# A two-layer kernel on one core: the opening's queues in another order

## The chip, the cores and the metric

The kernel runs on one core of a Trainium2 chip. The core's engines are TensorE (PE), VectorE (DVE), ScalarE (ACT), GpSimd (POOL) and SyncE (SP); each works through a queue of its own in order, and they meet at semaphores. The metric is the device time of one execution in microseconds; lower is better.

## The reference

Sixteen batches of x, each 512 rows of 512 columns, go through two layers with a residual each. Here is what is computed, cut to what matters:

```python
# layer 1, on h = layernorm(x); ctx is 16 x 512 x 1024
h = rmsnorm(h, g_res); h = einsum('bld,ed->ble', h, W_in) + b_in
h_patch = rmsnorm(ctx, g_init)[..., :512]
s = associative_scan(decay, h_patch)                    # a short-lived decay: a**k, a about 0.001
plug = clip(cumsum(boundary_mask(patch_lens)) - 1, 0, plen - 1)
x = x + s[plug] + h
# layer 2, on y = layernorm(x)
y_prev = y shifted by one row
xr = mu_r * y + (1 - mu_r) * y_prev;  xk = mu_k * y + (1 - mu_k) * y_prev
out = x + sigmoid(xr @ W_r.T) * (square(relu(xk @ W_k.T)) @ W_v.T)
```

## The kernel before

Every matrix is kept as a high part and a low part (`_hi`, `_lo`), and each product is three TensorE matmuls (lines 484 to 486): high by high and the two mixed ones. ScalarE makes the high part by a copy (`copy`, L704), VectorE the low part by a subtraction (`low`, L894). The host hands over x twice, in rows and turned (`in_x_turned`), so that the first projection needs no transposes.

A batch has four row tiles `t` and four column chunks `c` of 128. For a batch b the stages are: load of turned x (`xt`) and of x (`ring[b.slot]`, three buffers), their high and low parts (`x_hi`, `x_lo`), the projection with W_in (`project_tile`), the scan of the context rows (`stats_c`, `scan_input`, `u_high`, `u_low`, `scan`, `scan_out`), the store of the scan to the DRAM tensor `s_rows` (`store_scan`, from ScalarE's queue), then four indirect DMAs from POOL that add rows of `s_rows` to x (`add_rows`, L426, semaphores `dep_added`), then `add_x` (L1019), the statistics and the norm (`stats_b`, `norm_b`), the turn by transposes (`turn`, L588), the mixing with the previous row, and the gate, key and value products with W_r, W_k and W_v.

The loop is software-pipelined: `iteration(b)` of each engine works on b, b+1 and b+2. Before it stands an opening, written out by hand at the end of each engine's function, with batch 0's first layer and the preparation of the weights. The orders in it are what the change touches. In the opening, POOL makes a table of powers of the decay with 13 selects for each of its two halves (`make_decay`, L363), TensorE sums the weights' columns (L681), counts boundary marks with 64 small matmuls (`count_marks`, L660) and sums them (`sum_marks`, L672), and VectorE centres W_in (`centre`, L1144), takes running sums of the marks (`running_marks`) and makes the row numbers for the indirect DMAs (`patches`).

W_in is staged in `gate`, W_r in `turned`, W_k in `ring[2]`, W_v in `gate` again. Turned x of batch 0 and of batch 1 both go to `xt`, so batch 1's load waits on SP until batch 0's low parts are made (`xt_lo_ready`), and W_r's load stands behind it. The iteration for b = -1 (`is_first(nxt)` on VectorE, `first_steps` on TensorE) adds up batch 0, projects batch 1 and turns batch 0. `far` is a branch that this data does not take: every engine in it loads a flag from `far_table` and jumps over.

## Time and profile before

| | us |
|---|---|
| median of 3 runs | 786.25 (785.98 to 786.61) |
| the profiled execution | 788.05 |
| its span, first to last instruction | 786.5 |
| PE busy | 756.9 (96%) |
| DVE busy | 553.8 (70%) |
| ACT busy | 413.3 (53%) |
| POOL busy | 173.4 (22%) |
| mean granted TensorE clock | 0.986 of 2.4 GHz |

The chain of the whole profiled execution puts 85% of the span on PE, 4% on DVE, 4% on POOL and 1% on DMA. A start time is counted from the first instruction. A reader looks for the stretches in which PE is not busy, for the engine that it waits for there, and follows that engine's queue back.

### The profile page before, as it was taken

The numbers are of one execution on the slowest core, as the hardware profiler recorded it, in microseconds if no ns is written. First come the engines' busy times: TensorE is split into PE (matmuls) and PEld (weight loads), VectorE is DVE, ScalarE is ACT, GpSimd is POOL, SyncE is SP. The second block draws the span as 40 slices with busy tenths as digits, with TensorE's granted clock in tenths as the row PEclk, the third lists the DMA queues.
The fourth block names the chain that finished last, engine by engine and source line by source line (L and its number), as shares of the span: only waits on it lengthen the run. The fifth ranks groups of instructions, "written<-read, shape, count | busy, mean of one in ns | idle before, by whom it ended". The sixth has DMA issues, their size and how long they took to land.

```text
span 786.5 us, 11081 instructions
## 1 busy us (share of the span) xinstructions
PE 756.9 (96%) x3462; PEld 624.1 (79%) x3463; DVE 553.8 (70%) x1005; ACT 413.3 (53%) x681; POOL 173.4 (22%) x175
## 2 busy tenths in 40 slices
PE   7669899999999999999999999999999999999997
PEld 4457688888888888888888888888888888888876
DVE  4678797685866868586686858667685867667452
ACT  3317755454654645466464546656454665544760
POOL 7244131311213131121313112131311213130000
PEclk9879999999999999999999999999999999999999
DMA  7476153441706244170624417062441706231011
GB/s 256 150 188 166 60 124 132 112 143 47 209 2 167 88 110 144 46 208 0 156 98 109 144 43 211 0 166 88 108 146 41 212 0 160 94 102 20 1 54 54
DMA packets 42765, 85.73 MB, mean 109 GB/s; under 512 B 3536, under 2 KB 3536, under 8 KB 42704
## 3 DMA queue, kind: packets, MB, share of 16 engines
q1 hardware_dynamic: 30624, 63.71, 21.7%
q0 software_dynamic: 9216, 16.78, 13.5%
q10 hardware_dynamic: 2880, 4.76, 1.7%
q14 instruction: 31, 0.25, 0.1%
q8 instruction: 14, 0.23, 0.1%
HBM read 64.26 MB, written 21.76 MB: 109 GB/s over the span
## 4 chain that ended last, share of the span: by engine, by line
PE 85%; DVE 4%; POOL 4%; issue 2%; ACT 2%; DMA 1%; DVEq 0%; POOLq 0%; ACTq 0%
PE bank L484 27%; PE bank L486 27%; PE bank L485 27%; PE bank L588 3%; POOL ring L426 2%; DMA s_rows<-scanned 1%; POOL decay L363 1%; DVE xk_lo L894 1%; DVE scratch L989 0%; DVE ring L1019 0%; DVE gate L1044 0%; ACT scratch L794 0%; POOL rs_a L389 0%; DVE bn_a L923 0%; DVE bn_b L1025 0%
## 5 line engine op out<-in xcount | busy, mean ns | idle before, releaser
L426 POOL DMA_INDIRECT ring<-s_rows,patch_now x60 | 99.4, 1656 | 245.8 <-DMA s_rows<-scanned 214.6
L894 DVE TENSOR_TENSOR xr_lo<-scratch,xr_hi 128x512 fp32r<-128x512 f32 x124 | 85.6, 690 | 68.9 <-ACT xr_hi L704 68.4
L989 DVE SCALAR_TENSOR_TENSOR scratch<-turned,cols,scratch 128x512 f32<-128x512 f32 x128 | 94.6, 749 | 34.4 <-ACT scratch L749 15.0
L484 PE MATMUL bank<-wi_hi,xt_hi 128*128 128x512 f32 x256 | 104.0, 406 | 5.1 <-DVE xt_lo L894 5.1
L704 ACT ACTIVATE turned<-bank 128x512 f32<-128x512 f32 x64 | 33.4, 604 | 143.3 <-PE bank L588 114.7
L484 PE MATMUL bank<-xk_hi,wk_hi 128*128 128x512 f32 x256 | 99.9, 390 | 2.2 <-DVE xk_lo L894 2.2
L485 PE MATMUL bank<-wi_lo,xt_hi 128*128 128x512 f32 x256 | 101.8, 398 | 0.0
L486 PE MATMUL bank<-wi_hi,xt_lo 128*128 128x512 f32 x256 | 101.5, 396 | 0.0
L484 PE MATMUL bank<-wr_hi,xr_hi 128*128 128x512 f32 x256 | 99.7, 389 | 0.8 <-DVE xr_lo L894 0.8
L486 PE MATMUL bank<-xk_hi,wk_lo 128*128 128x512 f32 x256 | 99.6, 389 | 0.0
L485 PE MATMUL bank<-xk_lo,wk_hi 128*128 128x512 f32 x256 | 99.6, 389 | 0.0
L486 PE MATMUL bank<-wr_hi,xr_lo 128*128 128x512 f32 x256 | 99.6, 389 | 0.0
L485 PE MATMUL bank<-wr_lo,xr_hi 128*128 128x512 f32 x256 | 99.6, 389 | 0.0
L484 PE MATMUL bank<-wv_hi,xr_hi 128*128 128x512 f32 x240 | 94.0, 392 | 2.7 <-DVE xr_lo L894 2.7
L486 PE MATMUL bank<-wv_hi,xr_lo 128*128 128x512 f32 x240 | 93.4, 389 | 0.0
L485 PE MATMUL bank<-wv_lo,xr_hi 128*128 128x512 f32 x240 | 93.4, 389 | 0.0
L749 ACT ACTIVATE scratch<-turned,cols 128x512 f32<-128x512 f32 x128 | 89.5, 711 | 0.5
L704 ACT ACTIVATE xr_hi<-scratch 128x512 fp32r<-128x512 f32 x124 | 77.9, 628 | 20.4 <-DVE scratch L989 17.7
L781 ACT ACTIVATE gate<-bank 128x512 f32<-128x512 f32 x64 | 37.5, 595 | 83.3 <-PE bank L486 83.3
L1044 DVE TENSOR_TENSOR gate<-bank,gate 128x512 f32<-128x512 f32 x64 | 43.6, 688 | 53.2 <-PE bank L486 51.2
L395 POOL TENSOR_TENSOR rs_b<-v_b,half 128x4 f32<-128x4 f32 x16 | 16.5, 1034 | 230.5 <-DVE v_b L1031 230.5
L704 ACT ACTIVATE xk_hi<-scratch 128x512 fp32r<-128x512 f32 x64 | 40.4, 632 | 47.6 <-DVE scratch L989 46.8
(131 smaller groups left out, 1283.5 us busy)
## 6 DMA issues: line engine op xcount, KB each, us to landing
ring<-in_x SPq DMA_DIRECT2D x16, 1024.0 KB, 7.4
out<-gate SPq DMA_DIRECT2D x64, 256.0 KB
xt<-in_x_turned SPq DMA_DIRECT2D x15, 1024.0 KB, 5.2
ctx_rows<-in_ctx SPq DMA_DIRECT2D x16, 512.0 KB, 8.0
s_rows<-scanned ACTq DMA_DIRECT2D x16, 256.0 KB, 2.0
gate<-in_L_xattn_W_in SPq DMA_DIRECT2D x4, 256.0 KB, 3.4
xt<-in_x_turned SPq DMA_DIRECT2D x2, 512.0 KB, 6.3
turned<-in_L_ffn_W_r SPq DMA_DIRECT2D x1, 1024.0 KB, 7.8
```

The source lines that it names most:

```text
L395: nc.gpsimd.tensor_tensor(rs_b[:, :, 0], v_b[:, :, 0], half[:, :], ALU.pow).then_inc(rs_b_done, 1)
L426: pool.indirect_dma_start(ring[b.slot][:, t, :], None, s_rows[:, :], bass.IndirectOffsetOnAxis(ap=rows, axis=0), compute_op=ALU.add).then_ ...
L484: nc.tensor.matmul(where, lhs_hi, rhs_hi, start=start, stop=False)
L485: nc.tensor.matmul(where, lhs_hi, rhs_lo, start=False, stop=False)
L486: return nc.tensor.matmul(where, lhs_lo, rhs_hi, start=False, stop=stop)
L588: last = nc.tensor.transpose(first_bank(b, t)[:, tile(c)], normed[:, t, c * P:(c + 1) * P], ident[:, :])
L704: return nc.scalar.activation(to, of, ACT.Copy)
L749: nc.scalar.activation(scratch[:, i % 2, :], turned[:, c, 0:S], ACT.Copy, scale=cols[:, 3 + which, c:c + 1]).then_inc(carried, 1)
L781: nc.scalar.activation(gate[:, t, :], bank[4 + t][:, :], ACT.Sigmoid).then_inc(gate_ready, 1)
L894: return nc.vector.tensor_tensor(to, whole, high, ALU.subtract)
L989: nc.vector.scalar_tensor_tensor(scratch[:, 2 + i % 2, :], turned[:, c, 1:S + 1], cols[:, 1 + which, c:c + 1], scratch[:, i % 2, :], ALU.m ...
L1044: nc.vector.tensor_tensor(gate[:, t, :], bank[4 + t][:, :], gate[:, t, :], ALU.mult).then_inc(gated, 1)
```

## The change

Six edits, all in or for the opening. On SP, the load of the patch lengths comes first (it was on ScalarE's queue), the context load goes between the halves of turned x, turned x of batch 1 goes to `ring[2]` without a wait, W_r follows at once, and the load of W_k, whose buffer this is, waits for batch 1's low parts. On POOL, the second half of the decay table is 32 columns wide instead of 128, `root_c` goes ahead of it and of `ident`, and each `add_rows` waits for its own tile's statistics instead of all four. On TensorE, the scan stands after two tiles of chunk 1 instead of after chunk 1, and `sum_marks` after chunk 0 instead of chunk 2. On ScalarE, one small activation stands ahead of the wait for `cols`, the broadcasts of g and bias go ahead of it, and the copies have another order. On VectorE, the opening has another order, and in the first iteration each tile's `add_x` is followed by its statistics, ahead of `scan_input` and `u_low`. On all engines, `far` loads its second flag only inside the branch.

```diff
@@ SP, opening @@
+            sp.dma_start(lens[:, :], patch_lens).then_inc(lens_loaded, 16)
             for c in range(C):
                 load_part(staged[WIN], w_in, c, 1, win_loaded[c])
             load_part(xt, x_turned[0], 0, C // 2, xt_half_loaded)
+            load_ctx(Batch(0, 0))
             load_part(xt, x_turned[0], C // 2, C // 2, xt_loaded)
-            load_ctx(Batch(0, 0))
             load_x(Batch(0, 0))
             sp.dma_start(s_rows[P:S, :], x[0, P:S, :]).then_inc(s_filled, 16)
-
-            reached(sp, xt_lo_ready, Batch(0, 0), 2, 2)
-            load_xt(Batch(0, 1))
+            load_part(xt_of(Batch(0, 1)), x_turned[1], 0, C, xt_next_loaded)
             load_w(WR, w_r)
...
             load_x(Batch(0, 1))
+
+            reached(sp, xt_lo_ready, Batch(0, 1), 2, 2)
             load_w(WK, w_k)
@@ POOL, opening @@
-            make_decay()
+            make_decay(0, P, 0)
+            make_blocks()
+            pool.wait_ge(half_ready, 1)
+            root_c(Batch(0, 0))
+            assert len(powers) <= W32
+            make_decay(1, W32, P)
...
-            reached(pool, bn_a_done, Batch(0, 0), T, T)
             reached(pool, s_stored, Batch(0, 0), 16, 16)
             hold(pool, pool_passed)
             for t in range(T):
                 if t == T // 2:
                     root_a(Batch(0, 0))
+                pool.wait_ge(bn_a_done, t + 1)
                 add_rows(Batch(0, 0), t, patch_of[:, 0, t:t + 1])
@@ TensorE, opening @@
                 for t in range(T):
                     project_tile(Batch(0, 0), t, c)
-                if c == 1:
-                    pe.wait_ge(decay_lo_ready, 1)
-                    scan(Batch(0, 0))
-                if c == 2:
+                    if c == 1 and t == 1:
+                        pe.wait_ge(decay_lo_ready, 1)
+                        scan(Batch(0, 0))
+                if c == 0:
                     sum_marks()
@@ ScalarE, opening @@
-            act.dma_start(lens[:, :], patch_lens).then_inc(lens_loaded, 16)
             act.dma_start(cols[:, 0:3, :], columns.rearrange("p (n c) -> p n c", c=C)).then_inc(cols_loaded, 16)
             act.wait_ge(average_ready, 1)
+            nc.scalar.activation(v_b[:, 0, :], average[:, 0:1], ACT.Copy).then_inc(table_loaded, 1)
+            act.dma_start(g_ctx[:, :], g_init[0:D].partition_broadcast(P)).then_inc(g_ctx_loaded, 16)
+            act.dma_start(bias[:, :], b_in.partition_broadcast(P)).then_inc(bias_loaded, 16)
             act.wait_ge(cols_loaded, 16)
...
             x_hi(Batch(0, 0), 0)
-            weight_hi(WIN, 0, 1)
-            x_hi(Batch(0, 0), 1)
+            weight_hi(WIN, 0, 2)
             squares_c(Batch(0, 0))
-            weight_hi(WIN, 1, 2)
+            act.wait_ge(decay_ready, len(powers) + 1)
+            copy(decay_hi[:, 0, :], decay[:, 0, :]).then_inc(decay_hi_ready, 1)
             act.wait_ge(g_ctx_loaded, 16)
             nc.scalar.activation(g_ctx[:, :], g_ctx[:, :], ACT.Copy, scale=input_gain).then_inc(g_ready, 1)
+            x_hi(Batch(0, 0), 1)
             weight_hi(WIN, 2, 3)
             u_high(Batch(0, 0))
             weight_hi(WIN, 3, 4)
+            store_scan(Batch(0, 0))
             act.wait_ge(decay_ready, 2 * len(powers) + 1)
             copy(decay_hi[:, 1, :], decay[:, 1, :]).then_inc(decay_hi_ready, 1)
-            store_scan(Batch(0, 0))
+            x_hi(Batch(0, 1), 0)
             weight_hi(WR)
-            x_hi(Batch(0, 1), 0)
@@ VectorE, first iteration @@
                 if is_first(nxt):
                     stats_c(new)
+                    for t in range(T):
+                        add_x(nxt, t)
+                        statistics_b(nxt, t)
+                    stats_b(nxt, T)
                     scan_input(new)
                     u_low(new)
-                    for t in range(T):
-                        add_x(nxt, t)
-                    stats_b(nxt)
+                    norm_b(nxt)
                     scan_out(new)
                     far(new)
                     dve.sem_inc(far_over, 1)
-                    norm_b(nxt)
                     stats_a(new)
@@ VectorE, opening: the last steps @@
             x_lo(Batch(0, 1), 0)
-            weight_lo(WR)
+            weight_lo(WR, 0, 2)
             x_lo(Batch(0, 1), 1)
+            weight_lo(WR, 2, C)
```

SP's queue in the opening, ahead of the first output, as it was before. The names are tiles and inputs; `ring0` is x of batch 0, `ring1` of batch 1.

```order
L285 DMA xt<-in_x_turned 128x4x512 [waits xt_lo_ready]
L279 DMA turned<-in_L0_ffn_W_r 128x4x512
L288 DMA ctx_rows<-in_ctx_2048 128x1024 [waits far_over]
L282 DMA ring1<-in_x 128x4x512 [waits dep_added2,dep_added3,dep_added1,dep_added0]
L279 DMA ring2<-in_L0_ffn_W_k 128x4x512
```

The same place in the changed kernel:

```order
L299 DMA ring2<-in_x_turned 128x4x512
L287 DMA turned<-in_L0_ffn_W_r 128x4x512
L296 DMA ctx_rows<-in_ctx_2048 128x1024 [waits far_over]
L290 DMA ring1<-in_x 128x4x512 [waits dep_added2,dep_added3,dep_added1,dep_added0]
L287 DMA ring2<-in_L0_ffn_W_k 128x4x512 [waits xt_lo_ready]
```

Turned x of batch 1 has another buffer and no wait, and the wait for low parts stands at W_k's load.

VectorE's queue in the opening, from the low part of W_in's chunk 1 up to the statistics of batch 0's x, as it was before. `bn_a<-ring` are those statistics, `scanned` the scan's result, `patch_of` the row numbers.

```order
L894 TENSOR_TENSOR decay_lo<-decay,decay_hi 128x128
L947 SCALAR_TENSOR_TENSOR u<-ctx_rows,rs_c,g_ctx 128x512
L1144 SCALAR_TENSOR_TENSOR gate<-gate,cols,bank 128x512
L894 TENSOR_TENSOR u_lo<-u,u_hi 128x512
L894 TENSOR_TENSOR wi_lo<-gate,wi_hi 128x512
L894 TENSOR_TENSOR xt_lo<-xt,xt_hi 128x1024
L1144 SCALAR_TENSOR_TENSOR gate<-gate,cols,bank 128x512
L1172 TENSOR_SCALAR far_scanned<-bank 32x256
L1176 SCALAR_TENSOR_TENSOR far_scanned<-far_scanned 32x256
L894 TENSOR_TENSOR wi_lo<-gate,wi_hi 128x512
L905 TENSOR_TENSOR scanned<-bank,bias 128x512
L923 BN_STATS bn_a<-ring 128x6 x2
```

The same place in the changed kernel:

```order
L1191 TENSOR_SCALAR far_scanned<-bank 32x256
L1195 SCALAR_TENSOR_TENSOR far_scanned<-far_scanned 32x256
L908 TENSOR_TENSOR decay_lo<-decay,decay_hi 128x128
L955 TENSOR_SCALAR v_c<-v_c 128x1
L1163 SCALAR_TENSOR_TENSOR gate<-gate,cols,bank 128x512
L961 SCALAR_TENSOR_TENSOR u<-ctx_rows,rs_c,g_ctx 128x512
L1163 SCALAR_TENSOR_TENSOR gate<-gate,cols,bank 128x512
L908 TENSOR_TENSOR u_lo<-u,u_hi 128x512
L908 TENSOR_TENSOR wi_lo<-gate,wi_hi 128x512
L919 TENSOR_TENSOR scanned<-bank,bias 128x512
L1203 TENSOR_SCALAR patch_of<-bank 128x64
```

The scan's result no longer stands behind chunk 2 and 3 of turned x and W_in's last chunk; these now stand behind it.

VectorE's queue from the scale of the context rows of batch 1 (`v_c`) to the norm of batch 0, as it was before; `rs_a` scales the projection in the add.

```order
L941 TENSOR_SCALAR v_c<-v_c 128x1
L947 SCALAR_TENSOR_TENSOR u<-ctx_rows,rs_c,g_ctx 128x512
L894 TENSOR_TENSOR u_lo<-u,u_hi 128x512
L1019 SCALAR_TENSOR_TENSOR ring<-bank,rs_a,ring 128x512 x4
L1025 BN_STATS bn_b<-ring 128x6 x4
L1029 BN_AGGR mv_b<-bn_b 128x2 x4
L1031 TENSOR_SCALAR v_b<-mv_b 128x4
L905 TENSOR_TENSOR scanned<-bank,bias 128x512
```

The same place in the changed kernel:

```order
L955 TENSOR_SCALAR v_c<-v_c 128x1
L1034 SCALAR_TENSOR_TENSOR ring<-bank,rs_a,ring 128x512
L1039 BN_STATS bn_b<-ring 128x6
L1034 SCALAR_TENSOR_TENSOR ring<-bank,rs_a,ring 128x512
L1039 BN_STATS bn_b<-ring 128x6
L1034 SCALAR_TENSOR_TENSOR ring<-bank,rs_a,ring 128x512
L1039 BN_STATS bn_b<-ring 128x6
L1034 SCALAR_TENSOR_TENSOR ring<-bank,rs_a,ring 128x512
L1039 BN_STATS bn_b<-ring 128x6
L1047 BN_AGGR mv_b<-bn_b 128x2 x4
L1049 TENSOR_SCALAR v_b<-mv_b 128x4
L961 SCALAR_TENSOR_TENSOR u<-ctx_rows,rs_c,g_ctx 128x512
```

The adds are now paired with their statistics, and batch 1's scan input stands behind them.

## Rows read from the trace of the kernel before

**Rows 1.** Stretches: start:end, length, each engine's busy us (instructions), clock, DMA share, GB/s.

```profile
16.00:18.00 2.00, 2.00 (x8) 1.52 (x7) 0.89 (x2) 0.59 (x2) 1.39 (x4) 0.61 0.10 38
26.00:28.00 2.00, 1.38 (x3) 1.14 (x4) 1.89 (x4) 0.74 (x2) 0.00 (x0) 0.67 0.26 38
34.00:36.00 2.00, 0.84 (x4) 0.38 (x2) 0.85 (x7) 1.17 (x3) 0.00 (x0) 1.00 0.25 93
...
100.00:780.00 680.00, 678.79 (x3118) 565.32 (x3117) 482.31 (x859) 367.82 (x605) 133.58 (x109) 1.00 0.35 102
```

**Rows 2.** Waits of PE up to 110 us: waiter, releaser, us in total, times, longest.

```profile
PE bank L588 <- DVE normed L1038: 6.4, 1, 6.4
```

**Rows 3.** Timeline, ACT: start, us, engine line op names, count [idle before, releaser].

```profile
4.96 1.28 ACT L857 ACT_TABLE_LOAD   x1 [4.96 <-DMA cols<-in_L_xattn_g_res]
```

**Rows 4.** Timeline, PE, opening of batch 0.

```profile
6.71 5.12 PE L681 MATMUL bank<-gate,normed 128*128 128x512 f32 x8 [1.30 <-ACT normed L857]
11.76 3.86 PE L660 MATMUL bank<-scratch 128*32 128x16 bf16 x64
15.54 0.50 PE L484 MATMUL bank<-wi_hi,xt_hi 128*128 128x512 f32 x1
...
26.62 0.78 PE L484 MATMUL bank<-wi_hi,xt_hi 128*128 128x512 f32 x1 [0.71 <-DVE xt_lo L894]
...
28.47 0.63 PE L485 MATMUL bank<-wi_lo,xt_hi 128*128 128x512 f32 x1
...
31.15 0.21 PE L672 MATMUL bank<-far_scanned,above_block 32*128 32x64 bf16 x1
...
31.83 0.50 PE L484 MATMUL bank<-wi_hi,xt_hi 128*128 128x512 f32 x1
...
34.46 0.39 PE L486 MATMUL bank<-wi_hi,xt_lo 128*128 128x512 f32 x1
```

**Rows 5.** Chain that ended last, in order of time: start, us, what.

```profile
29.55 5.55 DMA s_rows<-scanned
...
55.28 6.16 DMA s_rows<-scanned
```

**Rows 6.** The same store's line, all sixteen batches.

```profile
DMA to landing us min/median/max: 2.0/2.0/6.2
```

**Rows 7.** Timeline, POOL: indirect DMAs of batch 0 (first, last) and batch 1 (first).

```profile
36.00 1.75 POOL L426 DMA_INDIRECT ring<-s_rows,patch_of  x1 [14.59 <-DMA s_rows<-scanned]
...
44.55 1.56 POOL L426 DMA_INDIRECT ring<-s_rows,patch_of  x1 [0.30 <-issue]
...
62.22 2.07 POOL L426 DMA_INDIRECT ring<-s_rows,patch_now  x1 [5.85 <-DMA s_rows<-scanned]
```

**Rows 8.** Timeline, DVE, from batch 0's low parts to its norm.

```profile
25.34 1.22 DVE L894 TENSOR_TENSOR xt_lo<-xt,xt_hi 128x1024 fp32r<-128x1024 f32 x1
...
28.84 0.67 DVE L905 TENSOR_TENSOR scanned<-bank,bias 128x512 f32<-128x512 f32 x1
...
31.94 0.22 DVE L1184 TENSOR_SCALAR patch_of<-bank 128x64 uint32<-128x64 f32 x1 [1.23 <-PE bank L674]
...
46.76 0.75 DVE L947 SCALAR_TENSOR_TENSOR u<-ctx_rows,rs_c,g_ctx 128x512 f32<-128x512 f32 x1 [3.93 <-POOL rs_c L400]
...
48.82 2.72 DVE L1019 SCALAR_TENSOR_TENSOR ring<-bank,rs_a,ring 128x512 f32<-128x512 f32 x4
51.45 2.46 DVE L1025 BATCH_NORM_STATS2 bn_b<-ring 128x6 f32<-128x512 f32 x4
...
54.48 0.17 DVE L1031 TENSOR_SCALAR v_b<-mv_b 128x4 f32<-128x4 f32 x1
...
56.18 1.92 DVE L1038 TENSOR_SCALAR normed<-ring,mv_b,rs_b 128x512 f32<-128x512 f32 x4 [0.93 <-POOL rs_b L395]
```

**Rows 9.** SP's issue of batch 1's x, and (DMA view, 40 to 60 us) W_v's landing.

```profile
49.68 0.37 SPq L282 DMA_DIRECT2D ring<-in_x  x1
```

```profile
gate<-in_L_ffn_W_v SPq DMA_DIRECT2D x1, 1024.0 KB, 11.7
```

More of the change, by code:

```diff
@@ L404, in far @@
                 n = far_count(pool, b)
-                with pool.If(n[0] > 0):
+                with pool.If(n > 0):
+                    earlier = far_earlier(pool, b)
                     for c in range(1, T):
-                        done = n[1] * (T - 1) + c
+                        done = earlier * (T - 1) + c
                         if c == 1:
@@ L463, in _ @@
                                     pattern=[[-1, P]], channel_multiplier=1).then_inc(ident_ready, 1)
-            pool.wait_ge(half_ready, 1)
-            root_c(Batch(0, 0))
             pool.wait_ge(patches_ready, 1)
@@ L514, in far @@
                 n = far_count(pe, b)
-                with pe.If(n[0] > 0):
+                with pe.If(n > 0):
+                    earlier = far_earlier(pe, b)
                     for c in range(1, T):
-                        done = n[1] * (T - 1) + c
+                        done = earlier * (T - 1) + c
                         if c > 1:
@@ L952, in far @@
                 n = far_count(dve, b)
-                with dve.If(n[0] > 0):
+                with dve.If(n > 0):
+                    earlier = far_earlier(dve, b)
                     for c in range(1, T):
-                        done = n[1] * (T - 1) + c
+                        done = earlier * (T - 1) + c
                         dve.wait_ge(far_loaded, done * 16)
@@ L1020, in add_x, with statistics_b, stats_b @@
                                                ring[b.slot][:, t, :], ALU.mult, ALU.add).then_inc(x2_ready, 1)
-            def stats_b(b):
-                for t in range(T):
-                    reached(dve, x2_ready, b, T, t + 1)
-                    nc.vector.bn_stats(bn_b[:, t, :], ring[b.slot][:, t, :]).then_inc(bn_b_done, 1)
+            def statistics_b(b, t):
+                reached(dve, x2_ready, b, T, t + 1)
+                nc.vector.bn_stats(bn_b[:, t, :], ring[b.slot][:, t, :]).then_inc(bn_b_done, 1)
+            def stats_b(b, first=0):
+                for t in range(first, T):
+                    statistics_b(b, t)
                 reached(dve, bn_b_done, b, T, T)
@@ L1199, in _ @@
             find_places()
+            x_lo(Batch(0, 0), 0)
             dve.wait_ge(cols_loaded, 16)
@@ L1203, in _ @@
             centre(0)
[L1204 to L1205 removed]
             centre(1)
[L1207 to L1208 removed]
+            weight_lo(WIN, 0, 2)
+            running_marks()
             dve.wait_ge(decay_hi_ready, 1)
             low(decay_lo[:, 0, :], decay[:, 0, :], f32(decay_hi[:, 0, :])).then_inc(decay_lo_ready, 1)
+            stats_c(Batch(0, 0))
+            centre(2)
             dve.wait_ge(g_ready, 1)
             scan_input(Batch(0, 0))
[L1213 removed]
+            centre(3)
             u_low(Batch(0, 0))
             weight_lo(WIN, 2, 3)
[L1216 to L1219 removed]
             dve.wait_ge(bias_loaded, 16)
             scan_out(Batch(0, 0))
[L1222 to L1227 removed]
+            patches()
+            statistics_a(Batch(0, 0), 0)
+            x_lo(Batch(0, 0), 1)
+            weight_lo(WIN, 3, 4)
+            stats_a(Batch(0, 0), 1)
             dve.wait_ge(decay_hi_ready, 2)
```

63 lines of the change are left out of this document (23 added, 40 removed).

## The prediction

> **What bounds the kernel now.** I read the stretches first. From 100 to 780 us PE is busy for 678.79 of 680 us [rows 1], and all the work there keeps its order, so whatever the change gives must come from the time before about 95 us. Next the waits of PE: in the opening it stands 6.4 us for batch 0's norm [rows 2], and it comes to chunk 2 of batch 0 late, at 26.62, for low parts of turned x [rows 4]. Then the chain that ended last. Up to 95 us it is not PE's: it goes through two stores of the scan to DRAM, 5.55 us from 29.55 and 6.16 us from 55.28 [rows 5], and the four indirect DMAs that wait for each. POOL's first of batch 0 starts at 36.00 and its first of batch 1 at 62.22 [rows 7]. After the second set come the root, the adds of batch 1, the last mixing, W_v's low parts and the gates, and then PE's unbroken stretch. So the end moves by as much as the indirect DMAs of batch 1 move, as long as nothing that stands beside them moves less.
>
> **Batch 0's projection starts earlier by 0.9.** ScalarE's table load stood behind the arrival of `cols`, 1.28 us from 4.96 [rows 3], and PE waited 1.30 us for its result [rows 4]. The small activation ahead of that wait takes the load out. I count 0.9 of the 1.30, since the first loads stand one DMA issue later on SP and VectorE's part before the marks is unchanged; the ends are 0 and 1.3. Batch 0's projection starts at 14.6 instead of 15.54 [rows 4].
>
> **The first store is issued at 22.8 instead of 29.55.** PE's queue: twelve matmuls after a pause, 4.5 (26.62 to 31.15), the sum of the marks 0.7 (31.15 to 31.83), six matmuls at 0.24 from start to start (31.83 to 34.46 is eleven of these), 1.4, the scan 0.9 (three matmuls at 0.24 and the last one's end), VectorE's `scanned` 0.7 [rows 4, 8]. That is 14.6 + 4.5 + 0.7 + 1.4 + 0.9 + 0.7 = 22.8. What the scan needs must be there by 21.2. The marks are counted at 14.5; behind them stand on VectorE two mark operations, a decay part, `v_c` and a centring, under 3 us together at no more than 0.75 each but for three small ones, then `rs_c` (no longer behind the second decay half on POOL), u at 0.75, and the copy and u's low part at about 0.7 each: some 19.5. That cover is 1.7 us deep; the smaller decay half, `root_c` in front and the lens load on SP cost and give nothing beyond it.
>
> **Its landing.** The store took 5.55 us while 2 MB of loads, turned x and W_r, stood beside it; the median of all sixteen batches is 2.0 [rows 5, 6]. These 2 MB now go out as the last two of SP's first twelve issues. The loads ahead of them had ended by about 17 (a DMA share of 0.10 from 16 to 18 us), and the 2 MB with the store lasted from about 27 to 35 (0.26 from 26 to 28, 0.25 from 34 to 36) [rows 1]. So they end at 22 to 24.5, when the store is just issued. I take 2.5, nearer to 2.0; the bounds are 2.0 and 5.6. It lands at 25.3, and POOL starts 0.9 later as before: 26.2 instead of 36.00 [rows 7]. The last of the four starts 8.55 later, at 34.7. Its rows are in by 39.9: SP's issue of batch 1's x, which waits for them, came 5.13 after the last start [rows 7, 9].
>
> **VectorE and PE take over as the bound for batch 0.** Behind `scanned` now stand the six small patch operations (at most 0.22 each, about 1.0), one tile's statistics 0.6, and the low part of turned x 1.2 [rows 8]: 25.6. PE waits for that one (as it did at 26.62), then 4.5 for chunk 2 and 3.0 for chunk 3 [rows 4]: 33.1. ScalarE's copy of batch 1's second half, which waits for this, takes 1.0 (an estimate, from 1.22 for the subtraction on as many elements [rows 8]): 34.1. Then on VectorE 1.2 for its low part, two weight parts at 0.6, `v_c`: 36.7. Before, this piece waited on the one buffer, `xt`, and on W_r's load ahead of the copies on ScalarE; both waits go. The four adds (2.72) and four statistics (2.46) follow in pairs [rows 8]: 41.9, with the last add at 40.6, so the rows at 39.9 are there. From the end of the statistics to the end of `v_b` it is 0.7 (53.91 to 54.65): 42.6 instead of 54.65.
>
> **The second store.** Now u, its copy and its low part stand ahead of the norm: 2.1 from 46.76 to 48.82 [rows 8], 44.7. The norm takes 1.9, `scanned` 0.7: 47.3, where the store was issued at 55.28 [rows 5]. It gains 8.0 only, since the norm moved in front of it. Beside it run 3 MB again: batch 1's x, W_k and W_v. These were issued from 49.68, W_v at about 50.65 with 11.7 to its landing [rows 9], so the last landed 12.7 after the first issue; now the first issue is at 39.9 and the end at 52.6. W_k's new wait on SP, for batch 1's low parts at 35.3, is over by then, and nothing is held by it. The store landed 0.9 ahead of W_v before, which gives 51.7; by its durations of 5.55 and 6.16 it would be 52.9 to 53.5. I take 52.4. Then 0.8 to POOL: 53.2 instead of 62.22 [rows 5, 7], a shift of 9.0.
>
> On this one place a rule can be weighed. The rows show 256 KB taking 5.55 and 6.16 us beside full queues, and 2.0 with little beside them [rows 5, 6]. The Trainium skill, DMA: Bandwidth & Descriptors, section Queues, rings and completion order, says that each DMA engine takes turns between the queue rows that have work, a packet at a time. By that, a store should get every second turn and need about twice its 2.0, that is 4.0, and land at 51.3, for a shift near 10.1. The rows are nearer to a third of the rate, and I go by them.
>
> **Beside the chain.** PE has batch 1's projection from about 34.1 to 42.2, stands until u's low part at 44.7, and turns batch 0 at 45.7 to 46.8 where it did at 56.88. This moves by 10 to 11, more than 9.0, so the gate product is not the last. The wait that VectorE then has for the root of batch 1 grows by about 1, in the shadow of the gate product at first and seen again at the key product; it is in the 9.0. The loads saved in `far` lie in the shadow of PE's queue, 1.2 us unbusy in 680 at the most [rows 1]: nothing. The wait per tile in `add_rows` gives nothing either, as the statistics of tile 0 are in at 24.4, before the store.
>
> **The sum.** 788.05 of the profiled execution less 9.0 is 779.05. It stands 1.80 above the median of the runs shown, 786.25; less 9.0 that is 777.2, my forecast. About 0.2% is what a measurement of this kernel can tell from no change. Its own range is 776 to 778.8.
>
> **The rivals.** Better service of the stores (rival 1): the second store lands before batch 1's statistics, which then release POOL at about 51.2 (the norm's end 46.6, `scanned`, the branch of `far` at about 1, four statistics 2.5, and the step to POOL). That is a shift of 11.0: 775.2. For it speaks the 2.0 of the other batches, against it that both stores with 3 MB or 2 MB beside them took over 5.5.
>
> The first store still pays (rival 2): the 2 MB last beyond 23, the store takes 5.6 and lands at 28.4. POOL starts at 29.3, the last add waits for its rows until 42.9 instead of 40.6, and the second store goes out at 49.6, the 3 MB end at 55.7. POOL comes at about 55.6: a shift of 6.6, 779.7.
>
> The early 2 MB share with what is needed first (rival 3), the weights, turned x and the context: at the 2 MB in 8 us of before that is up to 5.5 us on all the chain: 3.5 left, 782.7. Against it: they are issued last on SP's queue.
>
> Slower (rival 4), by the clock of TensorE. In the opening it sat at half level (1.2 GHz) after each pause: a matmul at 28.47 took 0.63 against 0.39 at 34.46 [rows 4]. The change makes a new pause, PE's from 42.2 to 44.7, just ahead of turn, gate and key products. If the clock stays at half through the gate and key products, 96 matmuls cost 0.24 more each, 23 us, and the time is 786.25 - 9.0 + 23 = 800. It decides from 38 matmuls on (9.0 / 0.24). Against it: after the pause that ended at 26.62 the full level was back by 34.46 at the latest, and the turn and the last tile of batch 1 stand between the new pause and the gate product.
>
> That the change does nothing (rival 5) would need the stores to keep their places: PE's first pause would have to move behind the scan.
>
> **How the numbers follow.** Forecast 0.60, rival 1 0.15, rival 2 0.15, rival 3 0.05, rival 4 0.03, rival 5 0.02. The range is from rival 1 with the table load's other 0.4 to beyond rival 2 with batch 0's projection unmoved (779.7 + 0.9 and a little): 774.8 to 781.0; rivals 3 to 5 are left out. Faster 0.95, same 0.02, slower 0.03.
>
> **What would show it.** Right: the first store near 22.8, POOL's first indirect DMA near 26.2 and batch 1's first near 53.2; `v_b` near 42.6; PE's wait before the turn under 3.5 us in place of 6.4; gate product some 10 earlier, PE unbroken from about 86. Wrong: a first store landing more than 3.5 us after its issue (rival 2), the first matmul of batch 0 after 15.5 (rival 3), matmuls of 0.63 in the gate product (rival 4), or a second store that lands in under 4 us (rival 1).

## The result, and the profile after

| | before | after |
|---|---|---|
| median, us | 786.43 (785.98 to 786.74, 4 runs) | 779.21 (778.86 to 780.35, 4 runs) |
| the profiled execution | 788.05 | 780.35 |
| its span | 786.5 | 778.8 |
| PE busy | 756.9 (96%) | 755.4 (97%) |
| DVE busy | 553.8 (70%) | 556.2 (71%) |

The ratio is 0.9911, with an interval of 0.9894 to 0.9928. The kernel is 7.2 us faster in the medians and 7.7 in the profiled executions; the forecast was 9.0. The median lies inside the range, 2.0 us above the predicted 777.2. It is also within 0.5 us of rival 2's 779.7, so the total time alone can't tell the forecast from that rival; the steps below do.

All of it comes from the opening. The turn of batch 1 starts at 95.37, where it started at 103.06, and from there to the end it is 683.4 us in both traces, as in those of all the experiments. The lines of PE's timeline that answer to [rows 4] (start, us, operation, idle time before it and its releaser):

```profile
5.20 4.11 PE L692 MATMUL bank<-gate,normed 128*128 128x512 f32 x4
9.49 1.96 PE L692 MATMUL bank<-gate,normed 128*128 128x512 f32 x4 [0.18 <-DMA gate<-in_L_xattn_W_in]
11.38 3.86 PE L671 MATMUL bank<-scratch 128*32 128x16 bf16 x64
15.87 0.72 PE L494 MATMUL bank<-wi_hi,xt_hi 128*128 128x512 f32 x1 [0.63 <-DVE wi_lo L908]
26.85 0.50 PE L494 MATMUL bank<-wi_hi,xt_hi 128*128 128x512 f32 x1 [2.10 <-DVE xt_lo L908]
46.17 0.47 PE L494 MATMUL bank<-u_hi,decay_hi 128*128 128x512 f32 x1 [4.56 <-DVE u_lo L908]
54.33 0.50 PE L494 MATMUL bank<-wr_hi,xr_hi 128*128 128x512 f32 x1 [1.00 <-DVE xr_lo L908]
```

The first two lines are the column sums, in two parts; the third is the marks. Batch 0's projection starts 0.33 later than before, where 0.9 earlier was forecast. The long wait of 6.4 for the norm [rows 2] is now one of 4.56 for u's low part, just ahead of the turn. The gate product starts 9.9 earlier (64.23 before), as forecast ("some 10").

The two stores, from ScalarE's queue, and the indirect DMAs of POOL that wait for them [rows 7]:

```profile
24.22 0.34 ACTq L757 DMA_DIRECT2D s_rows<-scanned  x1
48.48 0.33 ACTq L757 DMA_DIRECT2D s_rows<-scanned  x1
```

```profile
27.13 1.90 POOL L433 DMA_INDIRECT ring<-s_rows,patch_of  x1 [2.66 <-DMA s_rows<-scanned]
34.87 2.00 POOL L433 DMA_INDIRECT ring<-s_rows,patch_of  x1 [0.30 <-issue]
54.78 1.79 POOL L433 DMA_INDIRECT ring<-s_rows,patch_now  x1 [8.71 <-DMA s_rows<-scanned]
```

The first store is issued 5.33 earlier and takes 2.0; the second is issued 6.80 earlier and still takes 5.52. POOL's first indirect DMA of batch 1 moves by 7.4. The chain of the pieces that ended last, in order of time, now begins with turned x and goes through the context of batch 1 and the second store:

```profile
3.30 8.03 DMA xt<-in_x_turned
...
31.71 4.58 DMA ctx_rows<-in_ctx
...
48.48 5.52 DMA s_rows<-scanned
```

VectorE, between the two stores [rows 8]. The add and the statistics of a tile alternate as they were put, 1.38 us a pair:

```profile
31.79 0.17 DVE L1247 TENSOR_SCALAR cols<-cols 128x8 f32<-128x8 f32 x1 [1.69 <-issue]
...
37.50 0.15 DVE L955 TENSOR_SCALAR v_c<-v_c 128x1 f32<-128x1 f32 x1 [0.87 <-ACT ctx_squared L751]
37.61 0.75 DVE L1034 SCALAR_TENSOR_TENSOR ring<-bank,rs_a,ring 128x512 f32<-128x512 f32 x1
38.40 0.70 DVE L1039 BATCH_NORM_STATS2 bn_b<-ring 128x6 f32<-128x512 f32 x1
39.01 0.74 DVE L1034 SCALAR_TENSOR_TENSOR ring<-bank,rs_a,ring 128x512 f32<-128x512 f32 x1
...
43.80 0.17 DVE L1049 TENSOR_SCALAR v_b<-mv_b 128x4 f32<-128x4 f32 x1
43.88 0.75 DVE L961 SCALAR_TENSOR_TENSOR u<-ctx_rows,rs_c,g_ctx 128x512 f32<-128x512 f32 x1
```

### The profile page after: what moved, and what is told of

Read it like the earlier page. It is cut to its first block, busy times and chain, and to the rows that moved or that the text cites. A ratio compares the mean times of both kernels' runs of the same rounds, so it can differ in the third digit from the quotient of the medians.

```text
span 778.8 us, 10909 instructions
## 1 busy us (share of the span) xinstructions
PE 755.4 (97%) x3462; PEld 621.9 (80%) x3463; DVE 556.2 (71%) x1005; ACT 413.7 (53%) x682; POOL 175.5 (23%) x175
## 4 chain that ended last, share of the span: by engine, by line
PE 88%; DVE 4%; DMA 2%; issue 2%; ACT 2%; POOL 1%; SPq 0%; DVEq 0%; ACTq 0%; POOLq 0%
PE bank L494 28%; PE bank L495 28%; PE bank L496 28%; PE bank L599 3%; DMA xt<-in_x_turned 1%; POOL ring L433 1%; DMA s_rows<-scanned 1%; DMA ctx_rows<-in_ctx 1%; DVE ring L1034 1%; DVE xk_lo L908 1%; DVE scratch L1004 0%; DVE gate L1062 0%; ACT scratch L809 0%; DVE bn_a L937 0%; ACT scratch L807 0%
## 5 line engine op out<-in xcount | busy, mean ns | idle before, releaser
L433 POOL DMA_INDIRECT ring<-s_rows,patch_now x60 | 101.7, 1695 | 262.7 <-DMA s_rows<-scanned 231.0
L494 PE MATMUL bank<-wi_hi,xt_hi 128*128 128x512 f32 x256 | 102.1, 399 | 3.3 <-DVE xt_lo L908 2.7
```

Source lines behind the costliest of these rows:

```text
L433: pool.indirect_dma_start(ring[b.slot][:, t, :], None, s_rows[:, :], bass.IndirectOffsetOnAxis(ap=rows, axis=0), compute_op=ALU.add).then_ ...
L494: nc.tensor.matmul(where, lhs_hi, rhs_hi, start=start, stop=False)
```

## The experiments

Each kernel below is the changed kernel with one edit, if nothing else is said. "The changed kernel" in comparisons is its nine executions in two comparisons, 777.75 to 780.35, median 779.34. Times of before beside the experiments are 786.3 to 786.8.

**The changed kernel once more.** No edit. The execution profiled first had PE at half level (1.2 GHz) through part of the last product ahead of batch 1's turn; is that part of the change's cost?

> The changed kernel itself once more, beside the others, for its spread and for the half clock level that its first trace shows from 84.2 to 87.6 us in the value product. Theory A (the half level there came from pauses that fall differently from one execution to the next): this trace has it elsewhere or not at all, and its time is 0.6 us lower than 780.35 for the profiled execution. Theory B (it belongs to this kernel's order): it stands there again.

Measured: 779.43 (777.75 to 779.73). Between 84 and 88 us the stretches read (length, busy us of PE, PEld, DVE, ACT and POOL, clock, DMA share, GB/s), first of the execution above, then of this one:

```profile
84.00:88.00 4.00, 4.00 (x12) 3.14 (x11) 3.81 (x11) 2.84 (x4) 1.45 (x2) 0.57 0.00 0
```

```profile
84.00:88.00 4.00, 3.32 (x15) 2.41 (x14) 3.81 (x12) 2.54 (x4) 1.62 (x2) 1.00 0.01 2
```

The two executions are of one and the same program, so the dip does not belong to the order of the change (the first theory): here the clock is full from 52 on and the span 0.9 shorter (777.9), of which 0.3 was won before, at the root of batch 1 (61.45 for 61.76). The dip cost some 0.6.

**The broadcasts of g and bias.** The change moved them from about 6.3 to 1.83 on ScalarE's queue. Two kernels put them back, one behind the averages, one behind the copy of the first half of turned x. The edit of the second:

```diff
-            act.dma_start(g_ctx[:, :], g_init[0:D].partition_broadcast(P)).then_inc(g_ctx_loaded, 16)
-            act.dma_start(bias[:, :], b_in.partition_broadcast(P)).then_inc(bias_loaded, 16)
             act.wait_ge(cols_loaded, 16)
...
             x_hi(Batch(0, 0), 0)
+            act.dma_start(g_ctx[:, :], g_init[0:D].partition_broadcast(P)).then_inc(g_ctx_loaded, 16)
+            act.dma_start(bias[:, :], b_in.partition_broadcast(P)).then_inc(bias_loaded, 16)
```

> The changed kernel with ScalarE's two broadcast loads (g and bias) back behind the four averages, as they stood before the change, the small activation left where it is. In the changed kernel the first half of turned x landed at 11.35 where it had landed at 8.69. Theory A (the broadcasts take turns with W_in and turned x on the DMA engines): W_in's parts land in under 5 us in place of 6.2, the copy of turned x starts at 9.3 to 10.3, batch 0's projection at 14.5 to 15.2 instead of 15.87, and the time falls by 0.5 to 1.2 us. Theory B (it was the order on SP, with the context load ahead and longer issues): the copy still starts after 11 and the time stays within 0.3 us.

> The changed kernel with the two broadcast loads (g and bias) issued by ScalarE behind the copy of turned x's first half. With them one microsecond later only, W_in's parts landed in 3.2 us in place of 6.2, but turned x still came at 11.2. Theory A (the broadcasts take turns with whatever SP has under way): with neither beside it turned x lands at 8.7 to 9.5, batch 0's projection starts at 14.5 to 15.2 in place of 15.87, everything up to POOL's indirect DMAs comes 0.6 to 1.3 us earlier and so does the end; g is in time at 17. Theory B (the context load and lens on SP's queue hold it): turned x still comes after 11 and nothing moves.

Measured: 780.62 (779.6 to 781.18) behind the averages, where they go out only 1.1 us later than in the change: 1.3 more than the changed kernel, where the first theory had 0.5 to 1.2 less; 779.15 (778.51 to 779.68) behind the copy, the same as the changed kernel. ScalarE's copy of turned x, in the changed kernel and then with the broadcasts behind it:

```profile
11.35 1.06 ACT L715 ACTIVATE xt_hi<-xt 128x1024 fp32r<-128x1024 f32 x1 [7.22 <-DMA xt<-in_x_turned]
```

```profile
8.73 1.06 ACT L715 ACTIVATE xt_hi<-xt 128x1024 fp32r<-128x1024 f32 x1 [4.56 <-DMA xt<-in_x_turned]
```

The stretch from 4 to 6 us, of the changed kernel and of that with the broadcasts behind the copy:

```profile
4.00:6.00 2.00, 1.58 (x6) 1.03 (x7) 0.93 (x3) 0.13 (x1) 1.30 (x5) 1.00 0.97 210
```

```profile
4.00:6.00 2.00, 1.58 (x6) 1.04 (x7) 0.93 (x3) 0.17 (x1) 1.29 (x5) 1.00 0.98 322
```

The last two numbers are the DMA engines' busy share and the GB/s: equally busy, they move 210 in the one and 322 in the other (283 before). W_in's pieces land 6.2 us after their issue in the changed kernel, 3.6 with the broadcasts behind the copy and 3.4 before. So the early broadcasts are what delays turned x, by 2.6 us, and through it 0.8 us of the projection, which starts at 15.06. But the time does not follow. The first store is issued at 21.86, 2.4 earlier; then W_r, pushed back, is still under way (17.9 us to its landing for 14.9), the store takes 4.2 in place of 2.0, and POOL starts at 27.01 for 27.13. Most of the copy's gain is spent on that store. At batch 1 it shows once more and goes again: the second store is issued at 47.11, 1.4 earlier, but takes 6.0 in place of 5.5, and POOL starts at 53.92, 0.9 earlier; the four indirect DMAs and the root behind them then take 7.7 for 7.0, and the root is at 61.64 for 61.76. So the first theory holds up to the projection, and fails in the time.

In the first of the two kernels the delay of 1.1 us gave W_in its 3.2 but left turned x at 11.22: there the broadcasts fell on turned x instead. Why this kernel is slower than the changed one is not shown: up to POOL's start (26.89 and 54.72) it stands where the changed kernel does or 0.2 ahead, and falls behind in the indirect DMAs of batch 1, which take 7.9 us to the root (62.64); the turn of batch 1 starts at 95.64, for 95.37 and 94.45 in the changed kernel's two traces.

**The buffer of turned x.** It decides whether the 2 MB of turned x and W_r go out at once or behind batch 0's low parts. It was taken out of the changed kernel, and put alone into before:

```diff
-            return ring[2] if is_first(b, 1) else xt
+            return xt
...
+            reached(sp, xt_lo_ready, Batch(0, 0), 2, 2)
             load_part(xt_of(Batch(0, 1)), x_turned[1], 0, C, xt_next_loaded)
```

> The changed kernel with turned x of batch 1 back in the one buffer, and so its load and W_r's behind the wait for batch 0's low parts, all else as changed. Theory A (the free buffer matters through ScalarE's copies and VectorE's low parts ahead of batch 0's adds): the loads go out at 26.9, batch 1's copies end near 38 instead of 33.7, the adds start at 40 to 41 instead of 37.6, and the time rises by 2.5 to 3.5 us. The first store, issued at 24.2, has landed by then, so it gains nothing from the wait. Theory B (the free buffer only fills a pause, since the rows of the indirect DMAs bound the adds): the time rises by under 1 us.

> The kernel before with one edit of the change alone: turned x of batch 1 in ring[2], loaded with W_r without a wait, W_k's load behind batch 1's low parts. Theory A (the 2 MB that leave the store's side give their part): the first store, issued at 29.6, lands at 31.6 to 32 in place of 35.1, POOL's first indirect DMA starts at 32.4 to 33, the adds and the second store follow by the same, and the time falls by 3 to 3.8 us against the kernel before. Theory B (orders alone carry the gain): under 1 us.

Measured: 783.36 (782.93 to 784.68) without it, 4.0 more than the changed kernel, beyond the 2.5 to 3.5 of the first theory, which had the right cause; 785.59 (784.16 to 786.79, ten runs) for before with it, 0.7 less than before beside it, ratio 0.9993 (0.9983 to 1.0002). Out of the change the buffer is worth over half of the gain; on its own next to nothing is certain. By the time that is the second theory's result (under 1 us), though the first store did land in 2.0 as the first had it (issued 29.23). But POOL does not start at 32.4 to 33:

```profile
33.42 1.75 POOL L431 DMA_INDIRECT ring<-s_rows,patch_of  x1 [12.33 <-DVE bn_a L932]
...
58.64 1.63 POOL L431 DMA_INDIRECT ring<-s_rows,patch_now  x1 [5.57 <-DMA s_rows<-scanned]
```

The statistics of all four tiles hold it, and at batch 1 it stands 3.6 earlier than before. The profiled execution, 784.16, is the lowest of the ten, 3.9 under that of before; the others go up to before's own times. Why most of them do not keep the 3.6 stays open, as only the first has a trace.

**The wait per tile.** Each `add_rows` waits for its own tile's statistics. Back to all four:

```diff
+            reached(pool, bn_a_done, Batch(0, 0), T, T)
             reached(pool, s_stored, Batch(0, 0), 16, 16)
...
-                pool.wait_ge(bn_a_done, t + 1)
```

> The changed kernel with batch 0's indirect DMAs again behind all four tiles' statistics, which end at 29.2, where the first had started at 27.1. Prediction's claim: the wait per tile gives nothing, as the statistics of tile 0 are in before the store; the time stays within 0.3 us. Theory A (the later tiles' statistics end behind the store's landing, so the old wait would have held the first DMA): POOL starts at 29.4 in place of 27.13, the last rows land 1.5 to 2.2 us later, the last add waits for them by 0.5 to 1.2 us, batch 1's x with its store's company goes out 1.5 to 2.2 us later, and the time rises by 0.8 to 2 us.

Measured: 781.9 (781.56 to 782.72), 2.6 more than the changed kernel, more than either theory had.

```profile
30.09 1.75 POOL L433 DMA_INDIRECT ring<-s_rows,patch_of  x1 [5.68 <-DVE bn_a L937]
...
37.94 1.56 POOL L433 DMA_INDIRECT ring<-s_rows,patch_of  x1 [0.30 <-issue]
...
56.38 1.66 POOL L433 DMA_INDIRECT ring<-s_rows,patch_now  x1 [9.57 <-DMA s_rows<-scanned]
```

POOL starts 2.96 later, the rows arrive later, SP issues x of batch 1 at 42.49 for 40.78, the second store lands 1.6 later and the root of batch 1 comes 2.1 later (63.84). The prediction's "gives nothing" is refuted.

**The root ahead of the second decay half.**

```diff
-            pool.wait_ge(half_ready, 1)
-            root_c(Batch(0, 0))
             assert len(powers) <= W32
             make_decay(1, W32, P)
+            pool.wait_ge(half_ready, 1)
+            root_c(Batch(0, 0))
```

> The changed kernel with POOL's root_c of batch 0 behind the smaller second half of the decay table, as in the order of before. Theory A (the prediction: this part lies in a cover): POOL stood unbusy from 13.9 to 17.9, so the 13 selects end near 19.4 and the root at 19.9 instead of 18.45; u's low part then ends near 22.1, which is still ahead of TensorE's scan at about 22.6; the first store at 24.2 to 24.6, time unchanged within 0.5 us of the changed kernel, 778.9 to 779.8. Theory B (the root in front of the table is what lets the scan stand after two tiles of chunk 1): the first store 1.5 us or more later, near 25.7, all behind it later by as much, time 780.3 to 780.8.

Measured: 779.62 (779.12 to 780.47), the same as the changed kernel. The root came at 19.28, and PE waited 1.07 us for u's low part ahead of the scan (22.23), yet the store was issued at 24.00, not later than in the changed kernel (24.22). In this execution TensorE's clock made up for it. The stretch from 16 to 20 us, of the changed kernel, then of this one:

```profile
16.00:20.00 4.00, 4.00 (x11) 3.19 (x12) 3.69 (x8) 3.62 (x8) 1.68 (x5) 0.58 0.83 323
```

```profile
16.00:20.00 4.00, 4.00 (x23) 3.04 (x24) 2.37 (x7) 3.03 (x6) 3.00 (x10) 1.00 0.87 342
```

At full level (2.4 GHz) the twelve matmuls of chunk 0 need 2.9 us; in the changed kernel, mostly at half level, 4.5. So the root's cover is 1.85 deep at half level (20.7, the end of u's low part, to the scan at 22.55), and about 0.3 at full level: in the kernel with the old iteration below, which ran this stretch at full level, u's low part ends at 20.71 and the scan starts at 21.00. The edit should cost nothing in the one and up to 1.1 in the other (an estimate: here PE did wait 1.07, but the root behind was traced at full level alone).

**VectorE's first iteration in the order of before**, u and its low part ahead of the adds, all statistics behind all adds, the norm behind the scan's output:

```diff
+                    scan_input(new)
+                    u_low(new)
                     for t in range(T):
                         add_x(nxt, t)
-                        statistics_b(nxt, t)
-                    stats_b(nxt, T)
-                    scan_input(new)
-                    u_low(new)
-                    norm_b(nxt)
+                    stats_b(nxt)
                     scan_out(new)
...
+                    norm_b(nxt)
```

> The changed kernel with VectorE's first iteration in its old order: scan input and u's low part ahead of the adds, the four adds ahead of the four statistics, the scan's result ahead of the norm. Theory A (the end hangs on the second store, so its place in VectorE's queue counts): the scan input goes out at 38.5, the adds end near 43, statistics and v_b near 46.1 instead of 44.0, but the scan's result is taken right there, at 46.2 to 46.9, ahead of the norm, so the store goes out at 46.9 instead of 48.5 and lands 0 to 1.5 us earlier, while turn and gate product move 1 us later; the time falls by 0 to 1.2 us. Theory B (the norm and the turn carry the end): the time rises by 1 to 2 us.

Measured: 779.42 (778.73 to 779.57), the same as the changed kernel. The second store goes out at 47.08, 1.4 earlier, and lands at 52.39, as the first theory had it; PE turns batch 0 at 48.27, 0.9 later. In the trace some of it is left: POOL starts at 53.17 (54.78 and 54.40 in the changed kernel's two traces), the root of batch 1 is at 60.58 (61.76 and 61.45), and the span is 777.2, for 778.8 and 777.9. In the medians nothing of it is seen. This part of the change can be taken as neutral within the scatter.

**W_v behind the second store.** The store shares the core's DMA engines with 3 MB of loads. Here SP holds the last of them until the store has landed:

```diff
             sp.wait_ge(w_lo_ready[WIN], C)
+            reached(sp, s_stored, Batch(0, 1), 16, 16)
             load_w(WV, w_v)
```

> The changed kernel with one more wait on SP: W_v's load goes out only once batch 1's scan is stored. Theory A (the second store shares the DMA engines with the 3 MB of loads ahead of and beside it, and POOL's indirect DMAs of batch 1 carry the end): batch 1's x and W_k alone end near 49.6, so the store issued at 48.5 lands at 50.5 to 51.5 instead of 54.0, POOL starts at 51.3 to 52.3 instead of 54.78, and the time falls by 2.5 to 3.4 us. W_v then lands near 54, long before its first use at 69.5. Theory B (the store is slow of itself, a write to DRAM just after reads of it, whatever loads are about): the store still takes over 5 us and the time stays within 0.5 us. Theory C (another thing carries the end, such as the gate product's chain of turn and mixing): the store lands early but the time falls by under 1 us.

> The kernel with W_v's load held for batch 1's store once more, beside the two that build on it. Theory A (its gain over the changed kernel is real, 2.6 us by the trace): below 778.3 again, with POOL's first indirect DMA of batch 1 near 52.2. Theory B (the 1.3 us between the medians is their scatter): 779.0 to 779.6, like the changed kernel.

Measured: 777.9 (776.68 to 779.76) and 778.46 (777.26 to 779.78); the nine executions have the median 777.9, 1.4 under the changed kernel. That is less than the 2.5 to 3.4 of the first theory, though store and POOL stand where it had them. The second median lies between the two theories of its own expectation. The ranges overlap by 2 us, so the size of the gain is less certain than its sign. With 0.9891 and 0.9896 of before's time these are, beside the kernel with the broadcasts below (0.9883), the fastest of the study. The trace is plain, though. The store's line of the DMA view (KB, us to landing) and POOL's start, in the changed kernel and with W_v held:

```profile
s_rows<-scanned ACTq DMA_DIRECT2D x1, 256.0 KB, 5.5
```

```profile
s_rows<-scanned ACTq DMA_DIRECT2D x1, 256.0 KB, 2.6
```

```profile
52.20 1.63 POOL L434 DMA_INDIRECT ring<-s_rows,patch_now  x1 [6.03 <-DVE bn_a L938]
```

POOL starts 2.6 earlier, and the releaser is now the statistics of batch 1 (they end at 51.4): a second wait stands right behind the first. (In the second such kernel the store takes 2.3 and POOL starts at 52.07.) The indirect DMAs then run beside W_v and take 7.4 us from the first to the root (52.20 to 59.64), for 7.0.

**On top of it, the old first iteration, and the broadcasts behind the copy.**

> The changed kernel with W_v's load held for batch 1's store, and VectorE's first iteration in the order of before (scan and its low part ahead of the adds, the norm behind the scan's output). Theory A (with W_v held, batch 1's statistics and the store land together, and the old order moves the norm only from one side of the store to the other): the store is issued near 47.1 and lands near 49.7, but the statistics of batch 1 end near 51.9, and POOL's first indirect DMA comes at 52.0 to 52.6 as in the kernel with W_v held alone (52.20): time 777.4 to 778.4. Theory B (the old order gains its 1.6 us of the trace on top): POOL near 50.7, time near 776.3.

> The changed kernel with both earlier edits: the broadcasts of g and bias behind ScalarE's copies of the first half of turned x, and W_v's load held on SP until batch 1's store has landed. Theory A (the store's landing beside three queued loads is what holds batch 1's indirect DMAs in the broadcasts' kernel too, so the two gains add): the second store is issued near 47.1 and lands 2.6 later, near 49.7, as it did with W_v held; POOL's first indirect DMA of batch 1 near 50.7 instead of 53.92, batch 1's turn near 91.7, span near 775, time 776.0 to 777.0. Theory B (the time held by W_v and the broadcasts is the same time: the indirect DMAs' pace, or another wait such as TensorE's for the root, takes the second gain back): time as with W_v held alone, 777.9 or above, with the turn of batch 1 at 92.8 or later.

Measured: 779.22 (777.34 to 779.73) with the old iteration, 777.89 (777.11 to 778.56) with the broadcasts. Neither beats W_v's hold alone. With the old iteration the second store is issued at 46.18 and lands in 2.6, at 48.8, but the statistics release POOL at 51.81; the first theory's mechanism is seen, though its median lies 0.8 above what that theory gave. With the broadcasts g itself is late this time (it landed 8.72 us after its issue at 9.21, and u waited for it), and the first store goes out at 23.20, for 21.86 without W_v's hold. The second is issued at 49.27, as the load of batch 1's context took 6.8 us (4.6 in the changed kernel), and POOL starts at 52.83: the second theory holds, the gains do not add.

The kernel with the old iteration shows one thing more. Its profiled execution, 777.34, is 1.8 under its three others (779.13 to 779.73). Its opening is the changed kernel's, but its first store is issued at 22.68 instead of 24.22. The stretch from 16 to 20 says why:

```profile
16.00:20.00 4.00, 4.00 (x23) 3.04 (x24) 3.71 (x8) 3.64 (x7) 1.67 (x5) 1.00 0.84 328
```

Full level, as in the root's kernel. In seven other profiled executions with the changed kernel's opening up to there the clock is 0.57 to 0.60, and the store goes out at 24.2 to 24.4. So 1.5 us of the opening hang on whether TensorE drops to half level near 16. That this is also what separates the low from the high executions of a kernel is likely, and not shown.

## Why the prediction was right, and where it was off

**The mechanism was right.** The end moves with the indirect DMAs of batch 1, and these with the two stores. Forecast 9.0, in the profiled execution 7.7; step by step (the times are the profiled execution's):

- *The projection starts at 14.6*: it was 15.87, 1.3 late, and this is the step that failed, in two of its terms. The table load did leave ScalarE's wait (1.42 in place of 4.96 [rows 3]), and the column sums started at 5.20 in place of 6.71. But the two broadcasts that went in front with it, 256 KB each, took DMA time from W_in and turned x, which landed 2.6 later for ScalarE's copy. The prediction costed the activation and not the DMAs issued behind it, although it was they that were moved past the first loads. They explain 0.8 of the 1.3: with them behind the copy the projection starts at 15.06. The other 0.5 is in the column sums, whose length had been taken over from before. They started 1.5 earlier but took 6.2 us in place of 5.1, since the first four stood at about 1.06 us each and the later ones at 0.59. With the broadcasts behind the copy it was 6.1; why the first ones are slow is not shown.
- *The first store at 22.8*: 24.22, by the same 1.3 and 0.1 more. The pace of chunk 0 was right (4.5). The cover of u was there: its low part ended at 20.7, the scan started at 22.55.
- *It lands in 2.5*: 2.0. The 2 MB were over, at about 23.4. POOL 27.13 for 26.2.
- *Chunks 2 and 3 end at 33.1*: 32.6, though they began 1.2 later than forecast. Chunk 2 ran at full level, 2.8 us in place of 4.5: the half level of [rows 4] was carried over, and here it did not come. In the kernel with the old first iteration it did come behind the same pause of 2.1 (clock 0.72 from 26 to 28 us, 0.50 from 28 to 30), and `v_c` came at 37.70, so the full level was worth 0.2 at most: the wait for batch 1's context covered it.
- *`v_c` at 36.7*: 37.50. On this stretch two things had been left out. The branch of `far` stands on VectorE 1.69 us idle, and SP's load of batch 1's context waits for the end of it (31.71); the load took 4.58 beside the indirect DMAs, and ScalarE's squares waited for it (36.32). In before both lay in the cover of a later chain.
- *Adds and statistics 5.2, `v_b` at 42.6*: 5.6, and 43.80.
- *The second store at 47.3*: 48.48. From `v_b` on every step was as forecast (u to low part 2.1, norm 1.9, `scanned` 0.7).
- *It lands at 52.4*: 54.0. The 3 MB started at 40.78 for 39.9 (the last indirect DMA to SP's issue took 5.9, for 5.13 in [rows 7, 9]), ended at 53.45 for 52.6, and the store landed 0.5 behind them, not 0.9 ahead, 5.5 us after its issue where 5.1 was forecast. POOL 54.78 for 53.2, a shift of 7.4.
- Then the four indirect DMAs and the root took 8.75 to the first add, for 9.55 before: 0.8 given back, a shift of 8.2. The half level at 84 took about 0.5 to 0.6 of that in this execution: 7.7.

**The rule on the queues.** The second store's landings beside 3 MB are 5.5, 4.3, 5.7, 5.3, 6.3, 4.9 and 6.0 in seven traces of six kernels with the change's buffer, and 5.9 and 6.2 in the two without the change. By turns of one packet, as the Trainium skill has it (DMA: Bandwidth & Descriptors, Queues, rings and completion order), a store issued with 5 us of loads left would land in about 4.0, the prediction's estimate. One of the nine, 4.3, is near it; the others stay with the forecast's 5.1 or go beyond. No run changes the packets, so whether turns are taken is not shown.

**The rivals.** Rival 2 (the first store still pays) is out by its mechanism, since the store took 2.0, though its time came nearest to the measured one. Rival 1 (better service of the second) did not come by itself; the kernel with W_v held shows its mechanism: the statistics release POOL, at 52.20, where the rival had 51.2. It is worth 2.6 at POOL's start and 1.4 in the medians; between forecast and rival stood 2.0. Rival 3 had the right kind of cause with the wrong culprit: its sign came, a projection after 15.5, but turned x was late by other loads than the 2 MB, which cost 0.8. Rival 4: around the pause ahead of the turn the clock fell (0.79 and 0.60 on average from 44 to 52 us in the changed kernel's two traces) and was full from 52 on, before the gate product. Its price was too high besides: 0.24 is the difference of one matmul's length (0.63 for 0.39), but they overlap, and from start to start a matmul costs 0.43 for 0.23, so that 96 at half level would cost about 19 us and not 23. Its rule that half level comes after a pause does not fit the rows of before either: there the clock fell at 16.4, with PE busy without a break from 6.71 on.

Of its signs PE's wait before the turn ("under 3.5") missed, with 4.56: the turn waits for u's low part, and this came late with `v_c` and `v_b`.

**Said to give nothing.** For `far`'s loads no run tells. The root: nothing, as said. The small decay half has no run of its own. The wait per tile: 2.6 us, where the prediction said nothing. The comparison was with the wrong row. That tile 0's statistics were ready before the store only says that the new wait costs nothing; what the old wait would cost in the new order is the fourth tile's, 29.2, three us behind the store's landing.

## What to carry over

When a DMA is moved forward with the instruction in front of it, cost its bytes against the loads that it now overtakes: 512 KB of broadcasts held back turned x by 2.6 us, and moving them away again gave nothing in the end, mostly because the next transfer behind them was then late. A part that removes one wait of two that end together shows its worth only when the other goes too: the buffer gave 4.0 us within the change and at most 0.7 in the medians alone. Where a small store gates the next stage, hold back the bulk load that nobody needs yet rather than issuing the store earlier: here that was worth 1.4 us in the medians, an earlier issue nothing that they showed.

## What the runs showed of the hardware

**A store issued 4 us or more ahead of the end of another queue's loads landed when they ended.** In all nine traces with 3 MB on SP's queue beside it, these ended and the second store landed (us, from issue plus time to landing):

| kernel | store issued | W_v landed | store landed |
|---|---|---|---|
| before | 55.28 | 62.35 | 61.44 |
| before, buffer alone | 51.98 | 58.8 | 57.9 |
| after | 48.48 | 53.45 | 54.0 |
| after, once more | 49.32 | 53.2 | 53.6 |
| old first iteration | 47.08 | 53.1 | 52.4 |
| POOL waits for all | 49.30 | 55.45 | 55.6 |
| broadcasts behind copy | 47.11 | 52.65 | 53.1 |
| broadcasts behind averages | 48.24 | 53.3 | 53.9 |
| root behind | 48.50 | 52.8 | 53.4 |

In these nine it is within 0.9 us of the loads' end, whether it was issued 3.9 or 7.1 us before that. Issued closer to the end it lands later than the loads: with W_v held the 2 MB ended near 49.5, and a store issued at 48.66 landed at 51.3, in 2.6 us; with the broadcasts behind the copy the first store went out at 21.86 with W_r's landing at 24.5, and took 4.2. With nothing beside it, it takes 2.0. So an earlier issue (47.08 or 47.11) bought at most what the table shows. The mechanism behind this is not shown.

**Broadcast loads are dear beside others.** A 256 KB load of one vector to all partitions took 4.5 to 10.6 us in these kernels. While two of them ran in the changed kernel, from 4 to 6 and 6 to 8 us, the core moved 210 and 249 GB/s; with them behind the copy it moved 322 and 335, at a similar busy share of its DMA engines (0.97 to 0.98 for 0.98 and 0.92).

**The same stretch ran at either level of the clock.** From 84 to 88 us two executions of the changed kernel itself had a mean clock of 0.57 and 1.00, worth some 0.6 us. From 16 to 20 us, with the changed kernel's opening up to there, it was 0.57 to 0.60 in seven profiled executions (two of the changed kernel, five of experiments) and 1.00 in two, worth 1.5 us. In the seven PE had paused 0.46 to 0.64 us ahead of the projection; in the two the column sums had ended about 0.6 us later and there was no such pause. But before had none either and fell to 0.57 there, so the pause does not decide alone, and what does is open. The pause of 2.1 us that ends at 26.85 was followed by full level in both traces of the changed kernel (26 to 28: 1.00) and by 0.72 and then 0.50 with the old first iteration.

**The pace of indirect DMAs.** Four of them and the root behind took 7.0 to 7.9 us at batch 1 in the traces named here, and 7.6 before. What runs beside them does not order these times: 7.4 with W_v beside them, 7.9 in a kernel where it had already landed. What decides it is not shown. The spread of 0.9 us is as large as what several of the edits above are worth.
